# A delta rule solved from both ends without transition matrices, and rope partners side by side

## The reference

```python
x = layernorm(x + attention(x))       # 16 heads of 64, rms norm of x first, rope, window of 32 tokens back
x = layernorm(x + ffn(x))             # 128 -> 512 -> 128, relu
x = layernorm(x + delta_and_mlp(x))
x = layernorm(x + routed_ffn(x))      # light for all, heavy for 128 tokens, chosen by 50 steps of coordinate descent
```

```python
k = k / norm(k)
A = tril(k @ k.T, -1) + I
u = solve_triangular(A, v, lower=True)
y = (q @ k.T) @ (lr * u)              # = q @ G,  G = sum over tokens of k_t (lr_t u_t)^T
```

## Time and profile before

| | us |
|---|---|
| median of 3 runs | 486.85 |
| lowest and highest | 480.68, 499.92 |
| the profiled execution | 479.4 |
| its span, first to last instruction | 477.6 |
| TensorE busy in it | 404.4 (85%) |
| VectorE busy | 309.7 (65%) |
| ScalarE busy | 259.2 (54%) |
| GpSimd busy | 174.6 (37%) |
| mean granted TensorE clock, share of full | 0.959 |

### The profile page before, as it was taken

The page is one execution under the profiler, slowest core; times in us unless marked ns, Lnnn a source line. Parts: engine busy times, 40 slices in busy tenths (PEclk is TensorE's granted clock), DMA queues, the critical chain, the costliest instruction groups (busy, mean ns, idle before and its releaser), DMA issues.

```text
span 477.6 us, 18398 instructions
## 1 busy us (share of the span) xinstructions
PE 404.4 (85%) x7496; PEld 358.9 (75%) x7496; DVE 309.7 (65%) x1555; ACT 259.2 (54%) x654; POOL 174.6 (37%) x196
## 2 busy tenths in 40 slices
PE   2886999889998899988889985999996789889880
PEld 1775898879897799977757864998995477767670
DVE  1577876868768777767763679222035895888564
ACT  3244656556565565646473482346600448886937
POOL 2465433643454534543353557100005684000012
PEclk9997999989999999989999998899999799999986
DMA  6467365556666556656000000000000000000003
GB/s 231 114 144 179 83 155 124 125 147 152 159 159 160 146 134 157 179 130 149 19 2 0 1 0 3 4 4 3 0 1 1 0 2 1 1 3 2 0 2 88
DMA packets 20660, 35.38 MB, mean 74 GB/s; under 512 B 4512, under 2 KB 11680, under 8 KB 20576
## 3 DMA queue, kind: packets, MB, share of 16 engines
q1 hardware_dynamic: 20000, 33.16, 27.8%
q10 hardware_dynamic: 576, 1.05, 0.6%
HBM read 7.85 MB, written 1.05 MB: 19 GB/s over the span
## 4 chain that ended last, share of the span: by engine, by line
PE 60%; DVE 16%; ACT 7%; issue 6%; POOL 4%; SPq 3%; DMA 3%; ACTq 0%; POOLq 0%; DVEq 0%
PE QK L521 9%; PE VY L594 5%; PE O L572 4%; PE S L548 4%; PE PT L558 3%; PE O L663 3%; PE PT L581 3%; SPq L445 2%; PE S L740 2%; PE QK L721 2%; DVE unread_tests L1194 2%; PE S L735 2%; DMA t_swap<-t_sin 2%; POOL qk L1527 2%; PE S L756 2%
## 5 line engine op out<-in xcount | busy, mean ns | idle before, releaser
L1527 POOL TENSOR_TENSOR qk<-t_cos,t_swap 128x512 f32<-128x512 f32 x64 | 80.6, 1280 | 99.9 <-DMA t_swap<-t_sin 97.3
L1285 ACT ACTIVATE probs<-probs,negative_max 128x64 f32<-128x64 f32 x256 | 68.0, 338 | 44.0 <-DVE negative_max L952 43.1
L943 DVE TENSOR_TENSOR t_cos<-QK,cos 128x512 f32<-128x512 f32 x64 | 43.9, 685 | 32.0 <-PE QK L521 16.3
L1566 POOL TENSOR_TENSOR rstd<-var_eps,minus_half 128x4 f32<-128x4 f32 x24 | 25.4, 1057 | 100.3 <-DVE var_eps L996 95.6
L952 DVE CUSTOM_DVE_ANT_0 probs<-S,masks 128x64 f32<-128x64 f32 x256 | 39.4, 219 | 12.8 <-PE S L548 12.7
L943 DVE TENSOR_TENSOR t_sin<-QK,sin 128x512 f32<-128x512 f32 x64 | 43.5, 679 | 0.0
L521 PE MATMUL QK<-xnT,wq 128*128 128x128 f32 x256 | 36.8, 290 | 1.8 <-DVE t_sin L943 1.1
L1306 ACT COPY oT<-PT 128x512 f32<-128x512 f32 x32 | 18.7, 584 | 35.0 <-PE PT L581 34.9
L521 PEld LDWEIGHTS QK<-xnT,wq 128*128 128x128 f32 x256 | 33.6, 205 | 2.8 <-ACT xnT L1316 1.1
L594 PE MATMUL VY<-wo,oT 128*128 128x128 f32 x256 | 34.8, 280 | 0.7 <-ACT oT L1306 0.7
L572 PE MATMUL O<-v_before,probsT 64*32 64x65 f32 x1024 | 29.5, 229 | 7.0 <-issue 7.0
(11 more groups left out here) (277 smaller groups left out, 1100.3 us busy)
## 6 DMA issues: line engine op xcount, KB each, us to landing
t_swap<-t_sin SPq DMA_DIRECT2D x124, 128.0 KB, 2.5
v_before<-v_own SPq DMA_DIRECT2D x32, 132.0 KB
v_before<-v_own SPq DMA_DIRECT2D x62, 66.0 KB
late_tile<-late_weights SPq DMA_DIRECT2D x7, 189.0 KB
x_sb<-x SPq DMA_DIRECT2D x4, 256.0 KB, 4.6
out<-XA SPq DMA_DIRECT2D x4, 256.0 KB, 2.3
cos<-rope_cos SPq DMA_DIRECT2D x3, 256.0 KB, 3.5
sin<-rope_sin SPq DMA_DIRECT2D x3, 256.0 KB, 4.6
```

Source lines behind the costliest of these rows:

```text
L943: last = nc.vector.tensor_tensor(dst[:, u % G, PAIRS * j:PAIRS * j + PAIRS], QK[j][:].rearrange("p (m t) -> p m t", m=PAIRS), table[:, tok ...
L1285: last = nc.scalar.activation(probs[:, u % G, m, e, :], probs[:, u % G, m, e, :], ACT.Exp, scale=-1.0, bias=negative_max[:, u % G, e, m:m ...
L1527: nc.gpsimd.tensor_tensor(qk[:, h, c, WINDOW:WINDOW + P], t_cos[:, h, c], t_swap[:, h, c], ALU.add).then_inc(rope_done, 1)
L1566: nc.gpsimd.tensor_tensor(rstd[:, grp(q)], var_eps[:, grp(q)], minus_half[:, grp(q)], ALU.pow).then_inc(roots_done, 1)
```

## The change

Six edits. (1) The delta rule goes from both ends: the first eight blocks carry the state forward, the last eight carry an *adjoint* backward (how G depends on the state that enters there), eight rounds for both, joined by one product. No transition matrices: each round multiplies the state by the block's corrections, subtracts that from its values, and only then updates. Corrections of the first half are made transposed. (2) `normalise_x` is one multiplication by the broadcast rms. (3) The squares of the second and third group of 512 are made one block per unit, from 13 units before the group's first unit; the x loads come four units earlier. (4) The halves of a head are interleaved: channel i and its partner i+32 lie in neighbouring partitions, by reordering w_q (ScalarE, with the scaling) and w_k (GpSimd, new) after the load; the swap exchanges even and odd partitions, a side (q or k) at a time, with a semaphore each, two transfers a side, for unit 0 too. (5) The smaller parts of `stage_x` and `split_x` come one unit later. (6) The last constants are loaded at units 29 and 30 instead of 25 and 26.

```diff
-    return (np.concatenate([cos] * 4).astype(np.float32),
-            np.concatenate([sin, -sin, sin, -sin]).astype(np.float32))
+    partners = lambda a, b: np.tile(np.stack([a, b], 1).reshape(dim, tokens), (P // dim, 1)).astype(np.float32)
+    return partners(cos, cos), partners(sin, -sin)
...
+    MIDDLE = NB // 2
+    PAIR_ORDER = [p for k in range(MIDDLE // 2) for p in (k, NB // 2 - 1 - k)]
...
-            def swap_halves(u, sides=(0, 2)):
-                sp.wait_ge(rope_products_done, 2 * u + sides[1])
-                c = slice(PAIRS * sides[0], PAIRS * sides[1])
-                for r in range(0, P, D // 2):
-                    other = r ^ (D // 2)
-                    sp.dma_start(t_swap[other:other + D // 2, u % G, c], t_sin[r:r + D // 2, u % G, c]).then_inc(swapped[u % G], 16)
+            def swap_halves(u):
+                for j in range(2):
+                    sp.wait_ge(rope_products_done, 2 * u + j + 1)
+                    c = slice(PAIRS * j, PAIRS * j + PAIRS)
+                    for t in range(2):
+                        sp.dma_start(t_swap[1 - t:P:2, u % G, c], t_sin[t:P:2, u % G, c]).then_inc(swapped[u % G][j], 16)
...
-            swap_halves(0, (0, 1))
-            swap_halves(0, (1, 2))
+            swap_halves(0)
...
-                    if q > 1 and u == UG * q - 12:
+                    if q > 1 and u == UG * q - 16:
                         load_x(q)
...
+                if u == 29:
                     sp.dma_start(level_mask[:], level_dram).then_inc(ld_late, 16)
                     sp.dma_start(ident_squares[:], squares_dram).then_inc(ld_late, 16)
-                if u == 26:
+                if u == 30:
                     sp.dma_start(before[:], before_dram).then_inc(ld_late, 16)
...
-                pe.wait_ge(ld_qk[min(u, 1)], 32)
+                pe.wait_ge(wk_ordered, min(u, 1) + 1)
                 project_qk(u)
...
+            def correct(k):
+                wait(pe, corrections_kept, k - 1)
+                for i in range(2):
+                    n = 2 * PAIR_ORDER[k] + i
+                    to = B[k % 2][:, 256 * i:256 * i + 256]
+                    if n < MIDDLE:
+                        nc.tensor.matmul(to[:, 0:C], kv[:, n, 0:C], invT[:, n, :], start=True, stop=True)
+                        last = nc.tensor.matmul(to[:, C:], invT[:, n, :], kv[:, n, C:2 * C], start=True, stop=True)
+                    else:
+                        last = nc.tensor.matmul(to, invT[:, n, :], kv[:, n, 0:2 * C], start=True, stop=True)
                 last.then_inc(corrections_ps, 1)
...
+            def see(r):
+                n, last_n = r, NB - 1 - r
+                pe.wait_ge(corrections_kept, corrected(n))
+                pe.wait_ge(state_kept, r)
+                nc.tensor.matmul(B[2][:, 0:C], corrections[:, n, 0:C], state[:, r, :], start=True, stop=True).then_inc(values_ps, 1)
+                pe.wait_ge(adjoint_kept, r)
+                nc.tensor.matmul(B[4][:, 0:C], keys_T[:, last_n, :], adjoint[:, last_n + 1, :], start=True,
+                                 stop=True).then_inc(seen_keys_ps, 1)
+            def update(r):
+                n, last_n = r, NB - 1 - r
+                if r > 0:
+                    pe.wait_ge(values_kept, r)
+                else:
+                    pe.wait_ge(corrections_kept, corrected(n))
+                nc.tensor.matmul(B[3][:, 0:C], kv[:, n, 0:C], corrections[:, n, C:], start=True, stop=True).then_inc(state_ps, 1)
+                pe.wait_ge(corrections_kept, corrected(last_n))
+                wait(pe, seen_keys_kept, r)
+                nc.tensor.matmul(B[5][:, 0:C], corrections[:, last_n, 0:C], weighted_keys[:, last_n, :], start=True,
+                                 stop=True).then_inc(adjoint_ps, 1)
+                nc.tensor.matmul(B[7][:, 0:C], weighted_keys[:, n, :], corrections[:, n, C:], start=(r == 0), stop=False, ...)
+                nc.tensor.matmul(B[7][:, 0:C], weighted_keys[:, last_n, :], corrections[:, last_n, C:], start=False, stop=False, ...)
+            for k in range(3):
+                correct(k)
+            corrections_left = iter(range(3, NB // 2))
+            for r in range(MIDDLE):
+                if r > 0:
+                    see(r)
+                    for k in itertools.islice(corrections_left, 1):
+                        correct(k)
+                update(r)
+                for k in itertools.islice(corrections_left, 1):
+                    correct(k)
+            nc.tensor.matmul(B[7][:, 0:C], adjoint[:, MIDDLE, :], state[:, MIDDLE, :], start=False, stop=True, ...)
...
-                for n in range(GB * q, GB * q + GB):
-                    nc.vector.tensor_scalar(xn[:, n, :], x_sb[:, n, :], rms[:, n:n + 1], None, ALU.mult).then_inc(x_normalised, 1)
+                n = slice(GB * q, GB * q + GB)
+                nc.vector.tensor_tensor(xn[:, n], x_sb[:, n], rms[:, n].unsqueeze(2).broadcast_to([P, GB, C]),
+                                        ALU.mult).then_inc(x_normalised, 1)
...
+            for r in range(MIDDLE):
+                n, last_n = r, NB - 1 - r
+                if r > 0:
+                    dve.wait_ge(values_ps, r)
+                    nc.vector.tensor_tensor(corrections[:, n, C:], corrections[:, n, C:], B[2][:, 0:C], ALU.subtract).then_inc(values_kept, 1)
+                    dve.wait_ge(seen_keys_ps, r)
+                    nc.vector.tensor_tensor(weighted_keys[:, last_n, :], weighted_keys[:, last_n, :], B[4][:, 0:C], ALU.subtract).then_inc(seen_keys_kept, 1)
...
+                    last = nc.vector.tensor_tensor(state[:, r + 1, :], state[:, r, :], B[3][:, 0:C], ALU.add)
...
+                    last = nc.vector.tensor_tensor(adjoint[:, last_n, :], adjoint[:, last_n + 1, :], B[5][:, 0:C], ALU.add)
...
-                nc.scalar.mul(half(wq, h), half(wq, h), SCALE).then_inc(wq_scaled, 1)
+                nc.scalar.mul(partners(half(wq, h)), halves(half(wq_loaded, h)), SCALE).then_inc(wq_scaled, 1)
...
-                if u > 0 and u + 2 in XT_STEP:
-                    squares(XT_STEP[u + 2])
+                for q in range(2, TG):
+                    if 0 <= u - (UG * q - 13) < GB:
+                        square(GB * q + u - (UG * q - 13))
...
-                pool.wait_ge(rope_products_done, 2 * u + 2)
-                pool.wait_ge(swapped[h], 64 * (u // G + 1) + (64 if h == 0 else 0))
                 wait(pool, k_tail_kept, u - G + 1)
                 for j in range(2):
+                    pool.wait_ge(rope_products_done, 2 * u + j + 1)
+                    pool.wait_ge(swapped[h][j], 32 * (u // G + 1))
...
+            for h in range(G):
+                w = slice(h * GH * D, (h + 1) * GH * D)
+                pool.wait_ge(ld_qk[h], 32)
+                nc.gpsimd.tensor_copy(partners(wk[:, w]), halves(wk_loaded[:, w])).then_inc(wk_ordered, 1)
             pool.wait_ge(pool_step, 1)
             pool.wait_ge(qk_zeroed, 3)
```

139 lines of the change are left out of this document (72 added, 67 removed).

## The result

The changed kernel is faster. Its four executions have a median of 470.35 us (465.54 to 472.87) beside 492.88 for the kernel before (480.68 to 499.92): ratio 0.971, 95% interval 0.962 to 0.979. The ratios here leave out executions more than 1.5% above the fastest of their kernel, so they are not the quotients of the medians (0.954 here). Over all measurements of this study the medians are 473.1 us (12 executions) and 486.9 us (36), 14 us apart. The forecast was 465 us, from a sum of -17.2 us. The profiled execution took 469.3 us, only 10.1 less than that of before.

The account below looks back on a forecast made before the run. TensorE was taken to bound attention (174.0 of 193 us busy) and the delta rule's first parts, then a serial chain. Terms -8.3 - 1.0 - 1.6 - 2.1 - 1.6 - 1.2 - 1.0 - 0.4 = -17.2 gave 462; forecast 465, range 455 to 478 us.

Parts of the forecast that it names:

- sum of -17.2 us: Whole kernel: terms for delta rule, start, normalisation points, clock, loads and end added up; 462 us against the profiled 479.4.
- signs of being wrong: Late delta-rule rounds over 2.4 us, swap landing over 5 us, or TensorE idle staying near 19 from 35 to 228 us.
- The delta rule, -8.3: From 331.28 us to the copy of g: two chains without transitions take 21.1 us instead of 29.4; bounds -4 to -9.
- rounds 1 and 2: Delta rule: six products and two correction pairs each, set by TensorE, 3.2 us a round, 6.4 for both.
- the chain gives half: Rival, 0.13: VectorE instructions and products obstruct each other, clock falls; delta rule gives -4, attention -9: 466 to 468 us.
- The start, -1.0: Root 3.4 us later, given back at the swap; first scores stay at 23.0, unit 1 about 1 us ahead; bounds +1.5, -2.5.
- The two points of normalisation, -1.6, -1.2, -2.1 and -1.6: Attention: -1.6 at 35 us, -2.1 at 91 us; half clock behind them gives -1.2 (half counted) and -1.6.
- 0.69 or 1.9 and nothing between: Single multiplication by rms on VectorE: by the skill's rule alone, 0.69 or about 1.9 us per point; 1.3 taken.
- the third point: Third normalisation of 512 tokens in attention: TensorE did not wait there before, so no gain counted.
- The loads and the gap at 203.73, -1.0: TensorE's unexplained stop from 203.73 to 205.79 and its slow clock may hang on moved loads: 0 to -3.7, -1.0 taken.
- Attention in all: All terms outside the delta rule: start, normalisation points, clock, loads and last unit's sum; the prediction rounds them to -9.

Follow-up runs that it names:

- the two repeats: The changed kernel profiled again, second and third time, with no edit: attention's end 226.2 and 227.4 us, delta rule 20.6 both times, tail 122.1 and 125.4.
- the kernel before with the cover: Kernel before plus only small matmuls in TensorE's waits behind the copy of g, three ahead of each descent count wait included: median 482.5 us beside 486.1, ratio 0.988.
- eight transfers a unit: Changed kernel with rope partners 32 partitions apart again, four swap transfers per half unit, w_k copied in old order: executions of 530.95 and 547.44 us.
- two other kernels with the same cover: Kernel before with only these small matmuls, 475.9 to 484.9 us; changed kernel with them, root first, tables in pieces and later weight loads, 456.6 to 464.2 us.

## Why the prediction was right or wrong

The direction and the range were right (465, 455 to 478, against 470.35), the sum came close to the stages, and the size between whole executions was overstated. Of the signs of being wrong that it named, none appeared: late rounds of 1.83 us, a landing of 2.5, and TensorE idle for 16.7 us from 35 to 228 us instead of 19.0 (13.7 and 14.3 in the two repeats).

*The delta rule, -8.3.* Measured -8.8, within 0.1 in every profile. Product, hop and late round came out as derived from the earlier trace rows; rounds 1 and 2 took 3.10 us instead of 3.2. The fear that four VectorE instructions a round would stand in each other's way did not come true. So the rival "the chain gives half" is out, and this term was right by its mechanism.

*The start, -1.0.* -0.75 (mean of five first copies with the edits 32.1, without 32.8). Two errors cancel in part. The copy took 0.64, not 0.9, but the second had to wait for its half of w_k, so the root began at 9.52 (forecast 9.9). The first scores came at 25.62, not at 23: I had followed the rope sums and left out the value projections, which stand ahead of the scores on TensorE, with their split on VectorE.

*The two points of normalisation, -1.6, -1.2, -2.1 and -1.6.* The stalls went entirely, and so did the half clock behind the first, of which I had left half. Behind the second point the clock still fell in two of the five profiles with the edits, for 6.8 and 3.4 us from 96 us on, now beside the wait in the loop over keys. The multiplication took 0.68, 1.55 and 0.91 us at the three points; I took 1.3, within bounds of 0.69 and 1.9. At 85.17 it began 1.52 us into a pair of GpSimd sums that ended at 86.17, and itself ended at 86.72, 0.55 behind them; at 34.54 GpSimd's sum was over. The Trainium skill's rule ("SBUF — State Buffer", section "SBUF: two separate sides") holds in this row, VectorE waits until GpSimd's instruction is over. What I made of it, 0.69 or 1.9 and nothing between, was wrong, since it may start anywhere inside that instruction. My assigning the gain to one edit each was wrong too: one of them undone does not bring the stalls back in full.

A stall that the sum doesn't have went as well. The profile of before hardly shows it (0.31 us at 221.59), but in the four other profiles with before's attention it is 1.2 to 1.7 us, with the edits 0.3 or less. Here it is in the kernel before with the cover:

```profile
222.91 0.63 PE L581 MATMUL PT<-ident,o_sb 128*128 128x128 f32 x4 [1.67 <-ACT probsT L1300]
```

In two of those profiles TensorE also waited at the third point (0.71 and 1.46 us), which I had put at nothing. TensorE's waits of this kind went from 6.0 to 8.0 us in sum to 0.3.

*The loads and the gap at 203.73, -1.0.* The gap is there with the loads moved: 0.7 to 1.8 us against 1.0 to 2.1 in five profiles each. The earlier trace rows was one draw of something that varies between executions; -1.0 should have been about -0.3.

*Attention in all*: -8.9 forecast; 226.8 against 235.8, the means of five profiles each, -9.0. That the two agree so well is partly luck: the loads gave less than their term, the first stall and the one at 222 us more. Profile against profile it is -5.6, since the first profile of after was the latest of the five.

*The step that failed: how the sum was turned into a time, and the tail, which the sum has at nothing.* I set -17.2 against the profiled 479.4 and raised the result by 3 us for the spread of single executions. Before's own median was 486.85, 7.4 above the profiled one. Beside that median 465 is a change of -21.9, 4.7 more than the terms add up to; the same sum taken from the median gives 469.7, and 470.35 was measured (a near hit with some luck in it, since with a fourth execution before's median was 492.88). The stages that the change touches gave 17.8 us (8.8 and 9.0), but the two profiled executions are only 10.1 apart and the medians over all executions 14.

Of the 7.7 us that the two profiled executions lack, 4.2 are the tail and 3.4 the late end of attention in that execution. The tail took 117.0 us in all three of before. In the thirteen with the change or a part of it and the descent's own matmuls it took 121 to 133 us in twelve and 118.8 in the other. In the descent itself the clock fell in eleven of the thirteen. It did not in the first profile of after, nor with eight transfers a unit. In that first profile the descent ran as in before, and 1.0 of the 4.2 us were lost ahead of it and 3.2 behind it, where the clock was at 0.50 for longer. The descent of before, then of after:

```profile
395.00:440.00 45.00, 41.07 (x329) 33.78 (x327) 35.48 (x327) 37.30 (x51) 4.93 (x4) 1.00 0.01 1
```

```profile
380.60:425.60 45.00, 41.08 (x332) 33.89 (x332) 35.68 (x330) 38.01 (x51) 5.82 (x5) 1.00 0.01 2
```

I had looked for idle time only in the stages that the change touches. Yet TensorE's many small waits in the descent, 45.00 - 41.07 = 3.9 us of them, could be seen in before's own profile.

*What stays open.* How much of the 4 us between the stages' 17.8 and the medians' 14 the tail has is not shown. None of the three profiles of before has the clock falling in the descent, and two of them are among the fastest executions of that kernel. Over all executions the mean granted clock is nearly the same, 0.944 (32 of before) and 0.940 (12). With a cover in the tail alone it rose in before to 0.968 and more, so before very likely loses the clock in its tail too in other executions, though the cover's gain in time is not told from none. Whether it does so as often as the changed kernel, and why the clock falls at 53 us in one profile, at 73 in another and in neither place in a third, was not settled.

## What to carry to other kernels

Sum a forecast by stages, and compare stages, not ends: a stage that repeats within 0.1 us shows a gain that the whole time, wandering by 3%, hides. Turn the sum into a time from the same kind of number that will be measured: a median from a median, not from one profiled execution. Look at the granted clock in stages that the change doesn't touch, above all where another engine leads and TensorE has many small waits; three small matmuls ahead of some of them shortened the tail here by 6 us (123.0 to 116.7) and closed the executions up from 21 us apart to 1, though two other kernels with the same cover still lay 8 and 9 us apart. Follow every instruction that stands ahead of the released one on its engine, not only the one whose input comes earlier.

## What the runs showed of the hardware

Nine falls of the clock to 0.50 came with no wait of TensorE over 0.18 us in the 7 us before, all at nearly the same place in the program, 53 to 54 us behind the copy of g. They lasted 3.4 to 51.2 us with TensorE busy all but throughout. An issue on SyncE's queue costs 0.6 to 0.7 us whether it moves 64 or 128 KB, and with twice the transfers of half the size the kernel took 62 us more, of which the issues explain 45. A VectorE product with both inputs in SBUF took 0.68 us alone; begun inside a GpSimd sum it ended 0.55 us behind that sum (1.55 and 0.91 us in all).
